# Flamingo stack on one core: third mixture's routing in one pass, its last share straight to x, small inputs on ScalarE's queue, shared down products earlier

## The reference, cut to what matters

```
x = x + tanh(g_xattn[i]) * attention_i(layernorm(x), ctx)
x = x + tanh(g_ffn[i])   * ffn_i(layernorm(x))          # i = 0..3
```

```
scores = softmax(x @ gate_w.T); top_vals, idx = top_k(scores, 2)
for e in range(8):
    h  = silu(xs @ w1[e].T + b1[e])          # xs = token * weight of its choice
    x2 = h @ w2[e].T + b2[e]
    x3 = xs @ w3[e].T + b3[e]
    y  = y + sum(x2 * x3 * (idx == e))
z = (silu(x @ sw1.T) * (x @ sw2.T)) @ sw3.T    # shared products
return y + z
```

## Time and profile before

| | us |
|---|---|
| median of 3 runs (lowest, highest) | 611.07 (610.68, 612.0) |
| profiled execution | 612.51 |
| its span, first to last instruction | 610.4 |
| TensorE busy | 576.1 (94%) |
| VectorE busy | 383.7 (63%) |
| ScalarE busy | 378.7 (62%) |
| GpSimd busy | 231.1 (38%) |

### The profile page before, as it was taken

The page is one execution under the profiler, slowest core; times in us unless marked ns, Lnnn a source line. Parts: engine busy times, 40 slices in busy tenths (PEclk is TensorE's granted clock), DMA queues, the critical chain, the costliest instruction groups (busy, mean ns, idle before and its releaser), DMA issues.

```text
span 610.4 us, 10688 instructions
## 1 busy us (share of the span) xinstructions
PE 576.1 (94%) x3696; PEld 410.2 (67%) x3696; DVE 383.7 (63%) x742; ACT 378.7 (62%) x759; POOL 231.1 (38%) x216
## 2 busy tenths in 40 slices
PE   9899998899999989998898998999998899999997
PEld 6467767786655766776533444577777688888885
DVE  4578858566632657775245665388849566666665
ACT  4377776565565458887553444577775566666664
POOL 5006675582031100111001443000015688888884
PEclk9999998999999999999898999999999999999999
DMA  8300001331000000000000001000001466666640
GB/s 263 123 2 3 1 3 43 84 88 50 0 2 1 1 0 1 3 2 2 0 1 13 27 14 64 1 3 2 1 3 43 123 177 175 172 179 187 174 136 35
DMA packets 14851, 33.55 MB, mean 55 GB/s; under 512 B 2912, under 2 KB 8432, under 8 KB 14672
## 3 DMA queue, kind: packets, MB, share of 16 engines
q1 hardware_dynamic: 14800, 32.89, 18.6%
HBM read 32.03 MB, written 0.85 MB: 54 GB/s over the span
## 4 chain that ended last, share of the span: by engine, by line
PE 76%; DVE 8%; issue 6%; ACT 6%; POOL 3%; ACTq 0%; DVEq 0%; POOLq 0%
PE bank L779 8%; PE bank L781 8%; PE bank L780 8%; PE bank L689 5%; PE bank L700 4%; PE bank L715 3%; PE bank L654 2%; ACT wa L1334 2%; PE bank L663 2%; PE bank L1168 2%; PE bank L617 2%; PE bank L1193 2%; PE bank L1191 2%; PE bank L611 2%; PE bank L1058 2%
## 5 line engine op out<-in xcount | busy, mean ns | idle before, releaser
L490 POOL TENSOR_TENSOR h_lo<-wc,h_hi 128x512 fp32r<-128x512 f32 x56 | 72.8, 1304 | 17.6 <-ACT h_hi L1403 17.6
L779 PE MATMUL bank<-xn_hi,w_hi 128*128 128x512 f32 x168 | 66.0, 393 | 3.8 <-DVE wc L1820 2.0
L781 PE MATMUL bank<-xn_hi,w_lo 128*128 128x512 f32 x168 | 65.4, 389 | 0.0
L780 PE MATMUL bank<-xn_lo,w_hi 128*128 128x512 f32 x168 | 65.4, 389 | 0.0
L1844 DVE TENSOR_TENSOR wb<-arena,bank 128x512 f32<-128x512 f32 x64 | 44.0, 687 | 33.1 <-PE bank L781 33.0
L1403 ACT ACTIVATE h_hi<-wc 128x512 fp32r<-128x512 f32 x56 | 35.4, 633 | 42.3 <-DVE wc L1852 29.8
L1631 DVE TENSOR_TENSOR wa<-bank,row_max 128x512 f32<-128x512 f32 x64 | 44.2, 691 | 7.5 <-ACT wb L1280 4.3
L1280 ACT ACTIVATE wb<-wa 128x512 f32<-128x512 f32 x64 | 40.1, 630 | 13.8 <-DVE wa L1631 13.4
L482 POOL TENSOR_TENSOR w_lo<-ring,w_hi 128x384 fp32r<-128x384 f32 x42 | 42.7, 1020 | 15.3 <-ACT w_hi L1380 15.3
L1627 DVE TENSOR_REDUCE row_max<-bank 128x4 f32<-128x512 f32 x64 | 43.6, 681 | 6.3 <-PE bank L689 5.7
L583 POOL TENSOR_TENSOR cen<-cen,wc 128x512 f32<-128x512 f32 x16 | 20.8, 1300 | 63.4 <-DVE wc L2022 63.4
(11 more groups left out here) (325 smaller groups left out, 1346.7 us busy)
## 6 DMA issues: line engine op xcount, KB each, us to landing
arena<-comb_rows SPq DMA_DIRECT2D x64, 256.0 KB, 4.1
ring<-in_experts SPq DMA_DIRECT2D x42, 192.0 KB, 2.5
ring<-in_experts SPq DMA_DIRECT2D x8, 256.0 KB, 3.6
mats<-in_mats SPq DMA_DIRECT2D x1, 1472.0 KB, 10.1
mats<-in_mats SPq DMA_DIRECT2D x1, 832.0 KB, 6.3
mats<-in_mats SPq DMA_DIRECT2D x2, 320.0 KB, 8.1
x<-in_x_t SPq DMA_DIRECT2D x1, 512.0 KB, 3.8
context<-in_ctx_t SPq DMA_DIRECT2D x1, 512.0 KB, 4.6
```

The lines of the kernel that those rows point to most:

```text
L490: nc.gpsimd.tensor_tensor(h_lo[:, v % 3, :], hidden_of(v), h_hi[:, v % 3, :].bitcast(f32), ALU.subtract).then_inc(m_h_lo, 1)
L779: mm(out, w, x_, start=start, stop=False)
L780: mm(out, w, x_rest, start=False, stop=False)
L781: return mm(out, w_rest, x_, start=False, stop=stop)
```

## The change

1. Start: mask, cols and gates are loaded by three DMAs on ScalarE's queue, with a semaphore of their own (in_mask, now 48). keep_busy has 7 products instead of 11. Biases and mask come before the first normalisation, two K products before its spreading. The Q products use banks 5, 6, 4, 7 (Q_BANKS) and each waits for its own bank only.
2. First and fourth mixture: down(0) and down(1) stand between gate_up 3 and gate_up 4, with 2 + 4n and 2 + 2n idle products around them. turn_full writes banks 0 and 1.
3. Third mixture: one pick over all eight tiles directly after the exponentials; one pair of transposes behind the third pair of shared products; the first weight broadcast behind the fourth.
4. Its end: cen is added to x after 14 shares (add_experts), the last two shares go from wc straight to x (add_last). GpSimd adds 14 times instead of 16.
5. Exit: the output bias term is formed in expert unit 3, its evacuation in unit 5; the halves are centred one by one, the second half of V comes behind the spreading, and seven keep_warm products become two.

```diff
...
@@ -387,5 +387,2 @@
             load(mats0[:, :], a["mats0"], in_ctx)
-            load(cols[:, :], a["cols"], in_ctx)
-            load(mask_words[:, :], a["mask"], in_mask)
-            load(gates[:, :], a["gates"], in_mask)
             load(ident_bf[:, :], a["ident_bf"], in_consts)
...
@@ -575,3 +572,3 @@
                 nc.gpsimd.tensor_tensor(dst, dst, upd[:, 0:P], ALU.add).then_inc(x_updated, 1)
-            for e in range(8):
+            for e in range(7):
                 for c in range(2):
@@ -662,3 +659,9 @@
                         pe.wait_ge(a_q_rows, 8 * inst + m_ + 1)
-                    mm(bank[4 + m_][:, :], spread_w[:, 1, m_ * P:m_ * P + P], xn[:, c, :],
+                    elif inst == 0 and m_ < 3:
+                        pe.wait_ge(a_k_rows, m_ + 2)
+                    elif inst == 0:
+                        pe.wait_ge(tgb_ready, 3)
+                    elif m_ >= 2:
+                        pe.wait_ge(a_vtok, m_ + 1)
+                    mm(bank[Q_BANKS[m_]][:, :], spread_w[:, 1, m_ * P:m_ * P + P], xn[:, c, :],
                        start=True, stop=True).then_inc(a_q, 1)
...
@@ -816,4 +819,5 @@
                     pe.wait_ge(m_pick, n + 1)
+                    pe.wait_ge(m_silu, u0 + 5 + c)
                     for j in range(BH):
-                        last = nc.tensor.transpose(bank[6 + c][0:m["E"], j * P:j * P + P],
+                        last = nc.tensor.transpose(bank[c][0:m["E"], j * P:j * P + P],
                                                    routing(512, 2 * BH, m["E"])[:, BH * c + j, :], ident[:, :])
@@ -834,3 +838,7 @@
                     gate_up(v)
-                keep_warm(4 + 5 * n, bank[5])
+                keep_warm(2 + 4 * n, bank[5])
+                pe.wait_ge(m_score, 4 * n + 2)
+                for v in range(2):
+                    down(v)
+                keep_warm(2 + 2 * n, bank[5])
                 for v in range(4, 6):
@@ -844,6 +852,5 @@
                     weight(v)
-                for v in range(2):
-                    pe.wait_ge(m_fullE, 2 * n + v + 1)
-                    down(v)
                 for v in range(4, m["units"]):
+                    if v in (6, 7):
+                        pe.wait_ge(m_fullE, 2 * n + v - 5)
                     if v >= 6:
@@ -859,8 +866,4 @@
             pe.wait_ge(prepared, 1)
-            keep_busy(11, bank[7])
-            pe.wait_ge(prepared, 5)
-            norm_means(0)
-            for c in range(2):
-                norm_var(0, c)
-            pe.wait_ge(in_ctx, 48)
+            keep_busy(7, bank[7])
+            pe.wait_ge(in_mask, 48)
             pe.wait_ge(w_spread, 2)
@@ -872,4 +875,7 @@
                     .then_inc(a_mask_rows, 1)
+            pe.wait_ge(prepared, 5)
+            norm_means(0)
             for c in range(2):
-                norm_spread(0, c)
+                norm_var(0, c)
+            pe.wait_ge(in_ctx, 32)
             pe.wait_ge(w_spread, 4)
@@ -881,12 +887,16 @@
                     pe.wait_ge(a_k_rows, n - 2)
+                if 4 <= n < 7:
+                    pe.wait_ge(a_q_rows, n - 3)
                 k_rows_of(0, n, bank[4 + n % 3])
-            for n in range(4):
-                k0(n)
+            k0(0)
+            k0(1)
+            for c in range(2):
+                norm_spread(0, c)
+            k0(2)
+            k0(3)
+            pe.wait_ge(a_bias_rows, 1)
             bias_through_o(0)
             pe.wait_ge(w_spread, 6)
-            pe.wait_ge(a_k_rows, 4)
             pe.wait_ge(ln_out, 1)
-            pe.wait_ge(tgb_ready, 3)
             q_rows_of(0, 0)
-            pe.wait_ge(a_q_rows, 3)
             for n in range(4, 8):
...
@@ -1157,4 +1177,7 @@
                        start=True, stop=True).then_inc(e_x3, 1)
+                    if k == 2:
+                        for half in range(2):
+                            combine_t2(half)
                     if k == 3:
-                        combine_t2(0)
+                        weight(0)
                     if k >= 1:
...
@@ -1195,4 +1207,6 @@
                 if k == 0:
-                    combine_t2(1)
                     weight(1)
+                if k == 3:
+                    pe.wait_ge(e_z, 2)
+                    bias_through_o(1)
                 if k >= 1:
@@ -1204,12 +1218,15 @@
             i6 = NORM_OF[6][0]
-            pe.wait_ge(e_v, 16)
-            pe.wait_ge(e_z, 2)
-            bias_through_o(1)
+            norm_stats(i6, 0)
             attn_v(1, 0, bank[4])
-            attn_v(1, 1, bank[5])
-            pe.wait_ge(a_vtok, 4)
-            norm(i6, 3)
-            keep_warm(4, bank[5])
+            pe.wait_ge(e_u, 16)
+            norm_stats(i6, 1)
+            for c in range(2):
+                norm_var(i6, c)
+            keep_warm(2, bank[5])
+            for c in range(2):
+                norm_spread(i6, c)
             pe.wait_ge(tgb_ready, 4)
+            attn_v(1, 1, bank[7])
             pe.wait_ge(ln_out, 2 * i6 + 1)
...
@@ -1253,3 +1274,3 @@
                     act.wait_ge(a_q, 8 * inst + 4 * c + m_ + 1)
-                    fn(q_rows[:, m_, c * HALF:c * HALF + HALF], bank[4 + m_][:, :], ACT.Identity,
+                    fn(q_rows[:, m_, c * HALF:c * HALF + HALF], bank[Q_BANKS[m_]][:, :], ACT.Identity,
                        bias=bias_rows[:, m_, 4 * inst + 1:4 * inst + 2]).then_inc(a_q_rows, 1)
...
@@ -1451,4 +1472,6 @@
-            norm_means(0)
-            norm_rest(0)
+            for dst, src in ((mask_words, "mask"), (cols, "cols"), (gates, "gates")):
+                nc.scalar.dma_start(dst[:, :], a[src]).then_inc(in_mask, 16)
+            nc.scalar.preload_act_table(ACT.Sqrt)
             for c in range(2):
@@ -1456,3 +1479,4 @@
                 fn(mask_rows[:, c, :], bank[5 + c][:, :], ACT.Copy).then_inc(a_mask_out, 1)
-            act.wait_ge(in_mask, 32)
+            norm_means(0)
+            norm_rest(0)
             fn(tg[:, :], gates[:, :], ACT.Tanh).then_inc(tg_ready, 1)
...
@@ -1535,7 +1564,5 @@
                 fn(wb[:, k % 2, :], bank[k % 2][:, :], ACT.Silu).then_inc(e_sg, 1)
-            def weights2_out(c):
-                act.wait_ge(m_combT, 2 + c + 1)
-                fn(comb_t2[:, c * HALF:c * HALF + HALF], bank[4 + c][:, :].bitcast(bf16)[:, 0:HALF],
-                   ACT.Copy).then_inc(m_combE, 1)
-            weights2_out(0)
+                if k == 2:
+                    for c in range(2):
+                        weights2_out(c)
             act.wait_ge(e_sh, 4)
...
@@ -1556,6 +1581,10 @@
                 fn(sq[:, c, :], bank[2 + c][:, :], ACT.Identity, bias=col(B3 + e)).then_inc(e_x3b, 1)
-            for c in range(2):
-                v_token_major(1, c, bank[4 + c])
-            norm(NORM_OF[6][0])
+            i6 = NORM_OF[6][0]
+            nc.scalar.preload_act_table(ACT.Sqrt)
+            norm_square(i6, 0)
+            v_token_major(1, 0, bank[4])
+            norm_square(i6, 1)
+            norm_rest(i6)
             nc.scalar.preload_act_table(ACT.Exp)
+            v_token_major(1, 1, bank[7])
             q_rows_out(1, 0)
...
@@ -1890,5 +1910,4 @@
                 .then_inc(prepared, 1)
-            dve.wait_ge(in_mask, 32)
+            dve.wait_ge(in_mask, 48)
             v.tensor_scalar(mask_neg, mask_u8, -(2.0 ** 100), None, ALU.mult).then_inc(a_mask, 1)
-            norm_means(0)
@@ -1983,19 +2003,22 @@
+            score2, total2 = routing(0, TILES, 8), arena[:, 16384 + 2304:16384 + 2304 + TILES]
             def softmax_route(c):
+                tiles = slice(BH * c, BH * c + BH)
                 logits = bank[4 + c][:, :].rearrange("p (t e) -> p t e", t=4)[:, :, 0:8]
-                top = rt[:, 2 + c, 0:4]
+                top = total2[:, tiles]
                 dve.wait_ge(m_logit, 2 + c + 1)
                 link(v.tensor_reduce(top, logits, X, ALU.max))
-                v.tensor_tensor(grid(c, 8), logits, top.unsqueeze(2).to_broadcast([P, 4, 8]),
+                v.tensor_tensor(score2[:, tiles, :], logits, top.unsqueeze(2).to_broadcast([P, 4, 8]),
                                 ALU.subtract).then_inc(m_shift, 1)
-            def pick(c):
-                dve.wait_ge(m_score, 2 + c + 1)
-                score, total = grid(c, 8), rt[:, 2 + c, 0:4]
-                link(v.tensor_reduce(total, score, X, ALU.add))
-                link(v.reciprocal(total, total))
-                link(v.tensor_tensor(score, score, total.unsqueeze(2).to_broadcast([P, 4, 8]), ALU.mult))
-                rank = ranks(score, 8, earlier8, 4)
-                v.tensor_scalar(comb_pieces2[:, BH * c:BH * c + BH, 24:32], rank, 1.5, None, ALU.is_lt)
-                split_weights2(score, 8, c, 8).then_inc(m_comb, 1)
+            def pick():
+                dve.wait_ge(m_score, 4)
+                link(v.tensor_reduce(total2, score2, X, ALU.add))
+                link(v.reciprocal(total2, total2))
+                link(v.tensor_tensor(score2, score2, total2.unsqueeze(2).to_broadcast([P, TILES, 8]), ALU.mult))
```

(36 more changed lines are left out.)

55 lines of the change are left out of this document (26 added, 29 removed).

## The result

The change made the kernel slower: 617.06 us median of 8 executions (614.93 to 620.52) against 611.88 for the kernel before (8 executions, seven of them between 610.68 and 617.27 and one of 1417.36), ratio 1.0078, 95% interval 1.0051 to 1.0105. A ratio is not the quotient of two medians: it leaves out executions over 1.5% above the fastest of their kernel, and the medians do not. I had predicted 604.5, range 601.8 to 607.8. The profiled execution took 615.0 us, span 613.0, mean granted clock 0.989.

What follows compares the result with a forecast made beforehand. The chain of waits was taken as three quarters TensorE, so only its idle or slow stretches pay. Terms 4.9 - 0.25 + 2.9 - 2.4 + 1.4 = 6.55 off 611.07 gave 604.5 us, 8-in-10 range 601.8 to 607.8.

Steps and rivals of the forecast that it cites:

- Front: Third mixture, one early selection: 3.2 us from the chain and 1.7 from the clock, less 0.25 for the output-bias product.
- exit: End of third mixture: earlier adding to x and centring by halves start the queries 2.9 us sooner, range 1.2 to 3.2.
- its cover: Third mixture: the selection costs nothing under 5.5 us, since the shared product could not start before 311.02 anyway.
- Start: Start of kernel: earlier small inputs and reordered work gain 1.4 us, 0.6 to 2.2 by landing time.
- rival B: Start: TensorE stays on the low clock, costing 2.8 us, time 607.3; chance 0.17.
- The 0.22 of the warming matmuls: Start: warming matmuls took 0.22 us each, twice the later 0.11, read as the array still on its low level.
- What TensorE waits for is their landing ... I take 5.0: Start: the small inputs' landing, gates last, gates TensorE; taken as 5.0, between 4.15 and 5.8.
- the 5.8 that I had carried over from one queue: Start: late end for gates' landing, from its 4.0 us behind large inputs of its own queue; gain then 0.6.
- L: Start: large inputs hold the DMA engines, small ones land at 5.8; gain 0.6, time 605.3; chance 0.14.
- First and fourth mixture: Moved down products delay unit 4: losses of 1.4 and 1.0 us, together 2.4, range 0 to 2.8.
- rival D: Clock falls at all four: start (2.8), two waits before third down product (1.7 each), exit (1.7); 612.4; chance 0.04.

Runs made afterwards that it cites:

- s_warm_2: Repeat of s_warm, profiled again: changed kernel with the large mixtures of before and 26 warming passes instead of 14; 605.78 us.
- s_port: As s_sp, with GpSimd's clearing of the padded values held back until the mask operation is done; 604.74 us, ratio 0.9851 to the kernel before.
- m_fill: Changed kernel with the start of before and idle matmuls (6 and 10 passes) in the waits before both large mixtures' third down product; 610.67 us, ratio 0.9973.
- a_fill: Changed kernel with idle matmuls (14 and 22 passes) in the waits before the third down product of both large mixtures; 616.78 us, ratio 1.0074.
- after_2: The changed kernel unaltered, run once more for a profile of another execution; 620.35 us in its one execution.
- s_sp: Changed kernel with the large mixtures of before and the three small inputs in SyncE's queue ahead of x and the context; 610.73 us, ratio 0.9955.
- a_both_back: Changed kernel with the start and large mixtures of before, only the third mixture changed; 605.17 us, ratio 0.9889; repeated 604.11 us, 0.9844.
- s_warm: Changed kernel with the large mixtures of before and 26 warming passes instead of 14; 610.57 us, ratio 0.9934.
- b_banks_2: Repeat of: a_both_back with each of the first four Q products waiting only for its own bank; 607.04 us, ratio 0.9899.

## Why the prediction was wrong

**Third mixture, right.** Front predicted 4.65 net, measured 4.5 between the first profiles (2.8 chain, 1.7 clock where before had its fall); exit predicted 2.9, measured 2.8. The selection took 5.37 where I had 5.45, and stayed under its cover.

**Start, wrong by 5.1** (+1.4 predicted, -3.7 measured). Two steps failed. The larger one is rival B, the clock, which I left out of the sum with a chance of 0.17: I had priced it at 2.8, and it cost 3.2, as s_warm_2 shows. TensorE stayed on its lower clock (1.2 instead of 2.4 GHz: 3.78 for four centring products against 1.88). The 0.22 of the warming matmuls was the sign, and my argument against B, that TensorE would have worked 3.1 us by then, is refuted by s_port, where it had worked 5.7 us without idle time before the centring and was still slow. The other step is "What TensorE waits for is their landing ... I take 5.0". It landed at 6.97, beyond the 5.8 that I had carried over from one queue, since on the second queue gates took 5.3 instead of 4.0; with this late landing and the fast pitch s_warm_2 still lost 0.5, so landing and order together cost the other 1.9 of the 5.1. I had treated L and B as alternatives, and both came. I also missed the GpSimd clearing as a second gate at 6.9. The trace of before didn't show it as one: its clearing had ended at 6.67, and VectorE's mask operation waited until 7.70 for gates.

**First and fourth mixture, the chain right and the clock left out.** -1.4 and -1.0 predicted, -3.8 and -2.6 measured; the chain cost 1.2 to 1.4 and 1.0 (m_fill). The step that failed is the clock, put at nothing in the sum and left to rival D with a chance of 0.04: it fell behind these waits in 6 of 8 cases and cost 1.3 to 2.8 each. D's own sizes were off too: the waits before the third down product didn't grow to 2.2, they stayed at 0.8 to 0.9. And I argued that these gaps were half as long as the one in the earlier trace rows, looking at one wait at a time. In the first mixture of the changed kernel the waits are 0.80, 0.62 and 0.79, but from the end of the transposes at 116.4 to the third down product at 120.5 only the four matmuls of the broadcasts stand between them, 2.2 us of idle time in 4.2. Before the fall of the earlier trace rows it was 2.9 in 3.9 (322.2 to 326.1, these two waits and the 0.57 of the earlier trace rows), so the two stretches are alike:

```profile
323.87 0.40 PE L1144 MATMUL bank<-ident_bf,comb_pieces 128*128 128x128 bf16 x4 [1.63 <-DVE comb_pieces L1730]
...
324.96 0.39 PE L1178 MATMUL bank<-comb_t,select 128*128 128x512 bf16 x1 [0.69 <-ACT comb_t L1538]
```

The six down matmuls, 1.36 us, had stood in the middle of it. m_fill and a_fill show that filling the waits is enough to keep the clock. Why it stayed whole in 2 of the 8 cases with bare waits is open.

D demanded that all four places fall; three did (the exit did not), and with the start's late landing on top that was enough: 6.55 less 1.9 (landing and order), 3.2 (B), 2.4 and 1.6 (what the mixtures cost beyond the forecast) and 0.15 (third mixture) is -2.7.

**The sum.** 6.55 gained was forecast. By the stage table it is 7.4 gained in the third mixture, less 3.7, 3.8 and 2.6: -2.7 in the profiled executions. It is -5 in the medians; after_2 has a longer slow stretch in the start (4.5 more) and shows where the rest can lie, but the other executions have no profile, so this is not shown.

## What to carry to other kernels

Work that stands in a stretch of small products and waits also holds TensorE's clock: before moving it, count the matmuls left there, and price the move with the clock's share (here 1.3 to 2.8 a place) beside the chain's. When two rivals can both come true, give their sum a chance of its own. An input that is to come early must be issued ahead of the large ones, not beside them, and its consumer's engine must be free: ask which other instruction runs at that moment. Early inputs alone did not help the start here (s_sp), and work without idle time did not suffice for the fast pitch (s_port): read the pitch of the first large matmuls.

## What was not expected of the hardware

The clock column read 1.00 in the start of the changed kernel while matmuls ran at half pace (four centring products in 3.78 instead of 1.88); the pitch is the surer sign there. Whether a fall comes varies between executions of one kernel (before at 326 and 374; a_both_back at 298 and 10; s_warm at 10 and in the stage between). The fall near 298 stands in 12 of the 20 profiles; the most regular one is that behind the bare waits of the mixtures, 6 of 8. A fall costs one to several microseconds, and b_banks_2, whose start stage is 1.5 us shorter than a_both_back's, lost 4.3 to one in a later stage.
